# Edge scores of a graph attention layer: squares on ScalarE and a second product on TensorE for one of four chunks of dimensions

## The chip, the cores and the metric

One core of one Trainium2 chip. The metric is the device time of one launch in microseconds (us). TensorE, VectorE, ScalarE, GpSimd and SyncE run beside each other and meet at semaphores; sixteen DMA engines move data between HBM and the on-chip memory SBUF. TensorE writes to PSUM only.

## The reference, cut to what matters

The program is a block of a graph network: layer norm, a graph attention and a mixing term, and a mixture of experts. The change touches only the score of an edge in the graph attention (N = 2500 nodes, 80000 edges, 8 heads of 64 dimensions, 512 in all):

```python
def _gat_forward(x, edge_index, W_e, W_r, a):
    src = edge_index[0]
    dst = edge_index[1]
    h_e = jnp.einsum('nf,hfd->hnd', x, W_e)
    h_r = jnp.einsum('nf,hfd->hnd', x, W_r)
    a_src, a_dst, a_dif, a_abs, a_prd = jnp.split(a, 5, axis=1)
    s_src = jnp.einsum('hnd,hd->hn', h_e, a_src)[:, src]
    s_dst = jnp.einsum('hnd,hd->hn', h_e, a_dst)[:, dst]
    hr_src = h_r[:, src]
    hr_dst = h_r[:, dst]
    diff = hr_dst - hr_src
    score = s_src + s_dst + jnp.einsum('hed,hd->he', diff, a_dif) + jnp.einsum('hed,hd->he', jnp.abs(diff), a_abs) + jnp.einsum('hed,hd->he', hr_src * hr_dst, a_prd)
    alpha = jax.nn.leaky_relu(score, negative_slope=ALPHA)
```

With w = hr_dst - hr_src the product of the two rows is half of (hr_src^2 + hr_dst^2 - w^2). The two squares belong to the nodes and are put into tables beforehand. What is left for each edge, dimension and head is a_abs |w| - a_prd/2 w^2, which is -a_prd/2 (|w| - c) |w| with c = 2 a_abs / a_prd.

## The kernel before, in words

`score_edges` takes the edges, sorted by source node, in 336 groups of 256 (GROUP = 2 tiles of 128). For a group n, with its 512 dimensions in KF = 4 chunks of 128:

- GpSimd gathers the two tiles' target rows (512 dimensions and 8 head terms each) into `rows_v`, a ring of six (L1065). It waits for `summed` of six groups back.
- VectorE makes a one-hot matrix of source nodes, `source_onehot_t` (`locate`, L1094).
- TensorE expands the source rows with it into `ps_u`: for each tile two halves of 260 columns, in three bf16 parts each, 12 products in all (`expand`, L1133). A tile of `ps_u` is free once VectorE has subtracted from it in the group before.
- VectorE subtracts, in place in `rows_v`, one instruction for each tile (`differ`, L1100): this is w.
- TensorE transposes w, dimensions to partitions, in 8 pieces into `ps_w`, of which there is one (`transpose`, L1148). It waits for `abs_set` of the group before.
- ScalarE makes the magnitudes of all four chunks at once, `w_abs`, three buffers (`magnitudes`, L1178).
- VectorE makes z = (|w| - c) |w| with one instruction for each chunk (`multiply`, L1114; c is `corner`).
- TensorE sums over the dimensions of each head: for each chunk a product of `head_weight` (128x32, -a_prd/2 in the column of the head) with z, into that chunk's own strip of 32 PSUM partitions of `ps_heads`, and then for each of the two tiles a product that adds the head terms into strip 0 or 1 (`add_heads`, L1157 and L1160). It gives `summed`.
- ScalarE copies the scores out (`keep_scores`, L1183), and SyncE's queue writes them to HBM.

The order on each engine is written by hand: `in_turns` gives each step with how many groups it lags. The numbers set what stands behind what:

```python
in_turns(v, TURNS, ((2, differ_first), (2, differ_second), (4, multiply), (0, locate)), TURN)
in_turns(nc.tensor, TURNS, ((2, expand_first), (2, expand_second), (5, add_heads), (3, transpose)), TURN)
in_turns(sc, TURNS, ((9, magnitudes), (0, fetch_ids), (11, keep_scores)), TURN)
```

So TensorE goes, in turn m: expansion of group m-2, head sums of m-5, transposes of m-3; VectorE subtracts m-2, makes z of m-4, locates m.

Of the kernel before, what the change touches and what calls it, by code (L numbers as in the profile page):

```python
# [7 lines left out]
ALU = mybir.AluOpType  # L8
ACT = mybir.ActivationFunctionType
# [5 lines left out]
P = 128  # L15
L = 125
NB = N // L
KF = F // P
GROUP = 2
GE = GROUP * P  # L20
CHUNKS = P // HEADS
STRIP = P // KF
# [954 lines left out]
def score_edges(nc, a, const, edge, group_block, tab_v, parts, parts_in, scores, merged, keys, keys_in, local_ids):  # L977
# [7 lines left out]

    ident, row, col = const["ident"], const["row"], const["col"]
    BUFS, RING, TURN = 3, 6, 12
    ID_GROUPS, ID_SETS = 3, 4
    TURNS = GROUPS // TURN
    assert TURNS * TURN == GROUPS and GROUP == 2 and ID_GROUPS * ID_SETS == TURN  # L990
    HALF = EW // 2
    with ExitStack() as ctx:
        def sb(name, shape, dt=F32):
            return ctx.enter_context(nc.sbuf_tensor(name, shape, dt))
# [7 lines left out]
        def sbs(name, shape, dt=F32):  # L1002
            return [sb(f"{name}{h}", shape, dt) for h in range(BUFS)]
# [2 lines left out]
        ids = [sb(f"edge_ids{s}", [L, ID_GROUPS * GE], BF16) for s in range(ID_SETS)]  # L1006
        onehot_t = sbs("source_onehot_t", [L, GROUP, P], BF16)
        w, w_abs = rows, sbs("w_abs", [P, KF, GE])
        z = sbs("z", [P, KF, GE])
        score = sbs("score", [P, GE])  # L1010
        a_abs, prd, minus_prd = sb("a_abs", [P, KF]), sb("prd", [P, KF]), sb("minus_prd", [P, KF])
        tiny, corner = sb("tiny", [P, KF]), sb("corner", [P, KF])
        head_i, head_f = sb("head_i", [P, 1], I32), sb("head_f", [P, 1])
        head_sum, head_weight = sb("head_sum", [P, STRIP]), sb("head_weight", [P, KF, STRIP])
        ps_w = ps("ps_w", [P, KF, GE])
        ps_u = [ps(f"ps_u{j}", [P, 2, 512]) for j in range(GROUP)]

# [51 lines left out]
        def _(dve):  # L1069
            v = nc.vector  # L1070
# [11 lines left out]
            link(v.reciprocal(corner[:, :], prd[:, :]))  # L1082
            link(v.scalar_tensor_tensor(corner[:, :], corner[:, :], 2.0, a_abs[:, :], ALU.mult, ALU.mult))
            link(v.tensor_scalar(minus_prd[:, :], prd[:, :], -0.5, None, ALU.mult))
            for c in range(KF):
                ins = v.tensor_scalar(head_weight[:, c, :], head_sum[:, :], minus_prd[:, c:c + 1], None, ALU.mult)
            link(ins)
# [21 lines left out]
            def multiply(n, q, turn):  # L1109
                h = q % BUFS  # L1110
                at_least(dve, abs_set, n + 1)
                at_least(dve, summed, n - BUFS + 1)
                for c in range(KF):
                    ins = v.scalar_tensor_tensor(z[h][:, c, :], w_abs[h][:, c, :], corner[:, c:c + 1], w_abs[h][:, c, :], ALU.subtract, ALU.mult)  # L1114
                ins.then_inc(z_set, 1)

# [2 lines left out]
        @block.tensor  # L1119
        def _(pe):  # L1120
            pe.wait_ge(vectors_set, 1)
            pe.wait_ge(parts_in, 16 * PART_LOADS)

            block_of = {}

            def expand(n, q, j, b):

                at_least(pe, located, n + 1)
                at_least(pe, differed, n * GROUP + j - 1)
                for half in range(2):  # L1130
                    for part in range(PARTS):
                        rows_of_part = parts[:, DS(b, 1), part, half * HALF:(half + 1) * HALF].rearrange("p o c -> p (o c)")
                        ins = nc.tensor.matmul(ps_u[j][:, half, 0:HALF], onehot_t[q % BUFS][:, j, :], rows_of_part, start=part == 0, stop=part == PARTS - 1)  # L1133
                ins.then_inc(expanded, 1)

            def expand_first(n, q, turn):
                block_of[q] = pe.value_load(group_block[0:1, DS(n, 1)], min_val=0, max_val=NB - 1)
                expand(n, q, 0, block_of[q])

            def expand_second(n, q, turn):  # L1140
                expand(n, q, 1, block_of[q])

            def transpose(n, q, turn):
                at_least(pe, differed, n * GROUP + GROUP)
                at_least(pe, abs_set, n)
                for c in range(KF):
                    for j in range(GROUP):
                        ins = nc.tensor.transpose(ps_w[:, c, j * P:(j + 1) * P], w[q % RING][:, j, c * P:(c + 1) * P], ident[:, :])  # L1148
                ins.then_inc(turned, 1)

            def add_heads(n, q, turn):
                h = q % BUFS
                at_least(pe, z_set, n + 1)
                at_least(pe, score_kept, n - 1)
                for c in range(KF):
                    strip = ps_heads[q % 2][c * STRIP:(c + 1) * STRIP, 0:GE]
                    ins = nc.tensor.matmul(strip, head_weight[:, c, :], z[h][:, c, :], start=True, stop=True)  # L1157
                for j in range(GROUP):
                    strip = ps_heads[q % 2][j * STRIP:j * STRIP + HEADS, j * P:(j + 1) * P]
                    ins = nc.tensor.matmul(strip, w[q % RING][:, j, F:EW], ident[:, :], start=False, stop=True, skip_group_check=True)  # L1160
                ins.then_inc(summed, 1)

            in_turns(nc.tensor, TURNS, ((2, expand_first), (2, expand_second), (5, add_heads), (3, transpose)), TURN)

        @block.scalar
        def _(act):
# [7 lines left out]
            def magnitudes(n, q, turn):  # L1174
                h = q % BUFS
                at_least(act, turned, n + 1)
                at_least(act, z_set, n - BUFS + 1)
                sc.activation(w_abs[h][:, :, :], ps_w[:, :, :], ACT.Abs).then_inc(abs_set, 1)  # L1178

            def keep_scores(n, q, turn):  # L1180
                at_least(act, summed, n + 1)
# [812 lines left out]
```

## Time and profile before

| | |
|---|---|
| median of 3 runs | 3093.24 us (3088.78 to 3095.16) |
| the profiled execution's own time | 3089.13 us |
| its span, first to last instruction | 3087.2 us |
| mean granted TensorE clock | 0.923 |
| TensorE products busy | 2585.4 us (84%) |
| VectorE busy | 2339.1 us (76%) |
| GpSimd busy | 1500.3 us (49%) |
| ScalarE busy | 708.6 us (23%) |

The profile comes from one execution. PE is TensorE, PEld its weight loads, DVE VectorE, ACT ScalarE, POOL GpSimd. A busy time runs from an instruction's start to its end, latency included, and the ends of products are modelled; instructions of an engine can overlap at their ends. So two starts tell how fast an engine goes, and a duration tells when a result is there. In a timeline, instructions of one line that follow each other are merged: the row gives the first one's start, the time to the last one's end, and how many. Each f32 product has two records on TensorE. The stage that `score_edges` fills lies between about 580 and 1645 us.

### The profile page before, as it was taken

To read this page: it belongs to the slowest core of one execution; us is meant where nothing else is said; L and a number is where in the kernel's file an instruction comes from. 1 tells how busy PE (TensorE), PEld (TensorE's weight loads), DVE (VectorE), ACT (ScalarE), POOL (GpSimd) and SP (SyncE) were. 2 spreads that over 40 slices of the span, in tenths; PEclk is the share of its full clock that TensorE was granted. 3 is DMA by queue.
4 is the path that set the end of the run, shared out by engine and by line. 5 is a ranking of instruction groups with operands and counts; after the bars stand their busy time and mean duration, and the time that the engine had idled before them with its cause. 6 is when DMAs were issued, how large, how long until landed. Compare 5 with 4: busy or idle time off the path is not lost. (4 is left out here: it accounts for less than half of the span.)

```text
span 3087.2 us, 61474 instructions
## 1 busy us (share of the span) xinstructions
PE 2585.4 (84%) x16639; PEld 1699.8 (55%) x16640; DVE 2339.1 (76%) x4723; ACT 708.6 (23%) x1319; POOL 1500.3 (49%) x1562
## 2 busy tenths in 40 slices
PE   2399989599999999999992199999999998688990
PEld 2266654377777777777771154555555554675440
DVE  3567843499999999999998888888888888522111
ACT  0133331144444444444441100000000000331220
POOL 0233310366666666666660077777777776130113
PEclk6699989799999999999996599999999999689995
DMA  4012122777777777777774077777777776520224
GB/s 134 4 59 62 59 78 98 139 202 201 203 201 200 201 201 202 201 200 201 203 197 169 9 211 210 210 210 210 210 210 210 209 210 183 165 74 17 81 75 143
DMA packets 196487, 483.43 MB, mean 157 GB/s; under 512 B 51110, under 2 KB 81250, under 8 KB 195651
## 3 DMA queue, kind: packets, MB, share of 16 engines
q0 software_dynamic: 116400, 372.54, 44.5%
q1 hardware_dynamic: 55457, 84.04, 8.5%
q10 hardware_dynamic: 24562, 26.03, 2.6%
q8 instruction: 32, 0.52, 0.1%
q14 instruction: 36, 0.29, 0.0%
HBM read 435.38 MB, written 47.03 MB: 156 GB/s over the span
## 5 line engine op out<-in xcount | busy, mean ns | idle before, releaser
L1065 POOL DMA_INDIRECT rows_v<-target_rows,edge_dst x672 | 662.5, 986 | 413.5 <-PE ps_heads L1160 307.4
L1386 PE MATMUL ps_sum<-messages,node_onehot 128*125 128x512 f32 x1344 | 741.0, 640 | 77.6 <-DVE messages L1362 69.9
L1341 POOL DMA_INDIRECT rows_e<-message_rows,edge_dst x672 | 635.3, 945 | 346.4 <-issue 203.5
L1114 DVE SCALAR_TENSOR_TENSOR z<-w_abs,corner 128x256 f32<-128x256 f32 x1344 | 559.8, 478 | 1.3 <-ACT w_abs L1178 1.3
L1133 PE MATMUL ps_u<-edge_space,source_onehot_t 125*128 x4032 | 505.8, 275 | 32.9 <-DVE source_onehot_t L1094 28.6
L1178 ACT ACTIVATE w_abs<-ps_w 128x1024 f32<-128x1024 f32 x336 | 344.2, 1024 | 688.4 <-PE ps_w L1148 683.6
L1362 DVE TENSOR_TENSOR messages<-rows_e,ps_beside 128x1024 f32<-128x1024 f32 x336 | 410.2, 1221 | 103.4 <-DMA rows_e<-message_rows,edge_dst 97.8
L1100 DVE TENSOR_TENSOR rows_v<-rows_v,ps_u 128x520 f32<-128x520 f32 x672 | 456.1, 696 | 11.6 <-DMA rows_v<-target_rows,edge_dst 5.6
L1133 PEld LDWEIGHTS ps_u<-edge_space,source_onehot_t 125*128 125x128 bf16 x4032 | 393.6, 98 | 86.1 <-issue 34.4
L1387 PEld LDWEIGHTS ps_den<-edge_space,node_onehot 128*125 128x125 f32 x1344 | 253.1, 188 | 326.3 <-issue 326.3
L1148 PE MATMUL ps_w<-ident,rows_v 128*128 128x128 f32 x2688 | 367.3, 280 | 0.0
L1148 PEld LDWEIGHTS ps_w<-ident,rows_v 128*128 128x128 f32 x2688 | 287.7, 141 | 73.3 <-issue 72.3
L1386 PEld LDWEIGHTS ps_sum<-messages,node_onehot 128*125 128x125 f32 x1344 | 199.5, 188 | 104.8 <-DVE messages L1362 82.7
L1372 DVE TENSOR_TENSOR edge_space<-ps_sum,edge_space 125x512 f32 x336 | 229.5, 683 | 1.6 <-PE ps_den L1387 1.2
L1157 PE MATMUL ps_heads<-z,head_weight 128*32 128x256 f32 x2688 | 215.1, 392 | 2.6 <-DVE z L1114 2.6
L1401 ACT COPY ps_beside<-edge_space 128x96 f32 (+1 forms) x56 | 13.5, 243 | 805.6 <-DVE messages L1362 800.8
L1387 PE MATMUL ps_den<-edge_space,node_onehot 128*125 (+1 forms) x1344 | 189.5, 213 | 0.0
L1358 DVE TENSOR_TENSOR node_onehot<-ps_beside,edge_local 128x250 f32<-128x250 f32 x336 | 137.2, 408 | 0.4 <-ACT ps_beside L1401 0.4
L1799 DVE SCALAR_TENSOR_TENSOR swiglu_gate<-swiglu_gate,ps_up 128x256 f32<-128x256 f32 x27 | 11.4, 421 | 161.0 <-ACT swiglu_gate L1870 161.0
L354 POOL TENSOR_TENSOR squares<-row_v 125x512 f32<-125x512 f32 x20 | 20.9, 1044 | 228.6 <-ACT row_v L915 228.6
L1160 PE MATMUL ps_heads<-ident,rows_v 128*8 128x128 f32 x1344 | 130.8, 273 | 0.0
L1183 ACT COPY score<-ps_heads 128x256 f32<-128x256 f32 x336 | 123.0, 366 | 5.4 <-SPq L1053 3.6
(390 smaller groups left out, 2606.5 us busy)
## 6 DMA issues: line engine op xcount, KB each, us to landing
scores<-score SPq DMA_DIRECT2D x1344, 8.0 KB
edge_ids<-local_ids ACTq DMA_DIRECT2D x112, 187.5 KB
edge_space<-in_L_ffn_w_dram SPq DMA_DIRECT2D x24, 512.0 KB, 4.4
rows_v<-target_rows,edge_dst POOLq DMA_INDIRECT x672
rows_e<-message_rows,edge_dst POOLq DMA_INDIRECT x672, 3.7
source_parts<-edge_space SPq DMA_DIRECT2D x20, 380.9 KB
edge_space<-source_parts SPq DMA_DIRECT2D x4, 1904.3 KB
token_rows_out<-token_y SPq DMA_DIRECT2D x27, 256.0 KB, 2.8
```

The costliest lines, as they stand in the source:

```text
L1065: nc.gpsimd.indirect_dma_start(rows[q][:, j, :], None, tab_v, bass.IndirectOffsetOnAxis(ap=edge["dst"][:, tile:tile + 1], axis=0)).then_in ...
L1100: v.tensor_tensor(w[q % RING][:, j, :].rearrange("p (a b) -> p a b", a=2), rows[q % RING][:, j, :].rearrange("p (a b) -> p a b", a=2), ps_ ...
L1114: ins = v.scalar_tensor_tensor(z[h][:, c, :], w_abs[h][:, c, :], corner[:, c:c + 1], w_abs[h][:, c, :], ALU.subtract, ALU.mult)
L1133: ins = nc.tensor.matmul(ps_u[j][:, half, 0:HALF], onehot_t[q % BUFS][:, j, :], rows_of_part, start=part == 0, stop=part == PARTS - 1)
L1148: ins = nc.tensor.transpose(ps_w[:, c, j * P:(j + 1) * P], w[q % RING][:, j, c * P:(c + 1) * P], ident[:, :])
L1157: ins = nc.tensor.matmul(strip, head_weight[:, c, :], z[h][:, c, :], start=True, stop=True)
L1178: sc.activation(w_abs[h][:, :, :], ps_w[:, :, :], ACT.Abs).then_inc(abs_set, 1)
L1341: nc.gpsimd.indirect_dma_start(rows[q][:, j, :], None, tab_e, bass.IndirectOffsetOnAxis(ap=edge["dst"][:, tile:tile + 1], axis=0)).then_in ...
L1362: v.tensor_tensor(messages[h][:, :, :].rearrange("p j (h d) -> p (j h) d", d=D), rows[q % RING][:, :, :].rearrange("p j (h d) -> p (j h) d ...
L1372: v.tensor_tensor(total, ps_sum[q % BUFS][:, :], total, ALU.add)
L1386: nc.tensor.matmul(ps_sum[h][:, :], onehot[h][:, j, :], messages[h][:, j, :], start=j == 0, stop=j == GROUP - 1)
L1387: ins = nc.tensor.matmul(ps_den[h][:, 0:HEADS], onehot[h][:, j, :], tile_weights[:, DS(n * GROUP + j, 1), :].rearrange("p o h -> p (o h)") ...
```

## The change

Of the four chunks the last (SQUARED = 1) is no longer factored. ScalarE makes |w| of all four chunks as before and then w^2 of the last chunk in a second instruction; `abs_set` comes after both. VectorE makes z for three chunks. TensorE adds, in the last chunk's strip, `head_weight` times the squares and then a new `abs_weight` (a_abs in the column of the head) times the magnitudes. Since TensorE now reads `w_abs`, ScalarE waits for `summed` of three groups back before it writes there, where it waited for `z_set`.

```diff
+    SQUARED = 1
+    FACTORED = KF - SQUARED
...
-        z = sbs("z", [P, KF, GE])
+        z, w_square = sbs("z", [P, FACTORED, GE]), sbs("w_square", [P, SQUARED, GE])
...
+            for c in range(FACTORED, KF):
+                v.tensor_scalar(abs_weight[:, c - FACTORED, :], head_sum[:, :], a_abs[:, c:c + 1], None, ALU.mult)
...
-                for c in range(KF):
+                for c in range(FACTORED):
                     ins = v.scalar_tensor_tensor(z[h][:, c, :], w_abs[h][:, c, :], corner[:, c:c + 1], w_abs[h][:, c, :], ALU.subtract, ALU.mult)
...
-                    ins = nc.tensor.matmul(strip, head_weight[:, c, :], z[h][:, c, :], start=True, stop=True)
+                    if c < FACTORED:
+                        nc.tensor.matmul(strip, head_weight[:, c, :], z[h][:, c, :], start=True, stop=True)
+                    else:
+                        nc.tensor.matmul(strip, head_weight[:, c, :], w_square[h][:, c - FACTORED, :], start=True, stop=False)
+                        nc.tensor.matmul(strip, abs_weight[:, c - FACTORED, :], w_abs[h][:, c, :], start=False, stop=True)
...
-                at_least(act, z_set, n - BUFS + 1)
-                sc.activation(w_abs[h][:, :, :], ps_w[:, :, :], ACT.Abs).then_inc(abs_set, 1)
+                at_least(act, summed, n - BUFS + 1)
+                sc.activation(w_abs[h][:, :, :], ps_w[:, :, :], ACT.Abs)
+                sc.activation(w_square[h][:, :, :], ps_w[:, FACTORED:KF, :], ACT.Square).then_inc(abs_set, 1)
```

TensorE's order in one turn of the loop, before (with what a row waits for; lines L1133 expansion, L1157 and L1160 head sums, L1148 transposes, L1137 the next turn's table entry):

```order
L1133 MATMUL ps_u<-edge_space,source_onehot_t 128x260 [waits differed,located]
L1133 MATMUL ps_u<-edge_space,source_onehot_t 128x260 x5
L1157 MATMUL ps_heads<-z,head_weight 32x256 [waits score_kept,z_set]
L1157 MATMUL ps_heads<-z,head_weight 32x256 x3
L1160 MATMUL ps_heads<-ident,rows_v 8x128 x2
L1148 MATMUL ps_w<-ident,rows_v 128x128 [waits abs_set,differed]
L1148 MATMUL ps_w<-ident,rows_v 128x128 x7
L1137 TENSOR_LOAD group_block
```

The same turn now (expansion L1137, head sums L1162 to L1168, transposes L1152):

```order
L1137 MATMUL ps_u<-edge_space,source_onehot_t 128x260 [waits differed,located]
L1137 MATMUL ps_u<-edge_space,source_onehot_t 128x260 x5
L1162 MATMUL ps_heads<-z,head_weight 32x256 [waits score_kept,z_set]
L1162 MATMUL ps_heads<-z,head_weight 32x256 x2
L1164 MATMUL ps_heads<-w_square,head_weight 32x256
L1165 MATMUL ps_heads<-w_abs,abs_weight 32x256
L1168 MATMUL ps_heads<-ident,rows_v 8x128 x2
L1152 MATMUL ps_w<-ident,rows_v 128x128 [waits abs_set,differed]
L1152 MATMUL ps_w<-ident,rows_v 128x128 x7
L1141 TENSOR_LOAD group_block
```

Four products of 32x256 have become five; the fourth and the fifth write the same strip. Nothing else has moved.

ScalarE's order in the same loop, before (two turns):

```order
L1178 ACTIVATE w_abs<-ps_w 128x1024 [waits z_set,w_turned]
L1183 COPY score<-ps_heads 128x256 [waits score_free,summed]
L93 REGISTER_ALU
L1178 ACTIVATE w_abs<-ps_w 128x1024 [waits z_set,w_turned]
L1172 ISA [waits located]
```

And now:

```order
L1186 ACTIVATE w_abs<-ps_w 128x1024 [waits summed,w_turned]
L1187 ACTIVATE w_square<-ps_w 128x256
L1192 COPY score<-ps_heads 128x256 [waits score_free,summed]
L1186 ACTIVATE w_abs<-ps_w 128x1024 [waits summed,w_turned]
L1187 ACTIVATE w_square<-ps_w 128x256
L1180 DMA edge_ids<-local_ids 125x768 [waits located]
```

The squares stand between the magnitudes and the score copy of two groups before, without a wait of their own, and there is no table load in the loop.

## Rows read from the trace of the kernel before

**Rows 1.** The page, busy us (share of the span) and instructions.

```profile
PE 2585.4 (84%) x16639; PEld 1699.8 (55%) x16640; DVE 2339.1 (76%) x4723; ACT 708.6 (23%) x1319; POOL 1500.3 (49%) x1562
```

**Rows 2.** The page, busy tenths and granted clock in 40 slices of the span.

```profile
PE   2399989599999999999992199999999998688990
...
DVE  3567843499999999999998888888888888522111
...
PEclk6699989799999999999996599999999999689995
```

**Rows 3.** Busy time of each engine in one stretch, 700 to 1600 us.

```profile
core 0: us, PE busy (x) PEld busy (x) DVE busy (x) ACT busy (x) POOL busy (x), PEclk, DMA share, GB/s
700.00:1600.00 900.00, 900.00 (x9209) 673.55 (x9206) 900.00 (x2014) 370.68 (x576) 565.94 (x576) 1.00 0.75 201
```

**Rows 4.** Groups of instructions by line, 700 to 1600 us, shapes kept apart.

```profile
line engine op names shapes xcount | busy us, mean ns | idle before us <-releasers
...
L1114 DVE SCALAR_TENSOR_TENSOR z<-w_abs,corner 128x256 f32<-128x256 f32 x1150 | 479.1, 478 | 0.0
...
L1148 PE MATMUL ps_w<-ident,rows_v 128*128 128x128 f32 x2297 | 313.7, 280 | 0.0
L1178 ACT ACTIVATE w_abs<-ps_w 128x1024 f32<-128x1024 f32 x288 | 295.0, 1024 | 530.5 <-PE ps_w L1148 530.5
...
L1157 PE MATMUL ps_heads<-z,head_weight 128*32 128x256 f32 x2304 | 184.0, 391 | 0.0
...
L1183 ACT COPY score<-ps_heads 128x256 f32<-128x256 f32 x288 | 105.5, 366 | 0.0
```

**Rows 5.** Who waited for whom, 700 to 1600 us: total, times, longest.

```profile
ACT w_abs L1178 <- PE ps_w L1148: 530.5, 288, 1.9
POOL rows_v L1065 <- PE ps_heads L1160: 245.2, 288, 0.9
...
PEld ps_w L1148 <- issue: 62.7, 287, 0.2
PEld ps_heads L1157 <- issue: 61.6, 288, 0.2
```

**Rows 6.** Timeline of TensorE's products, 1199.8 to 1203.7: start, us, what.

```profile
1199.56 1.09 PE L1148 MATMUL ps_w<-ident,rows_v 128*128 128x128 f32 x8
1200.49 1.49 PE L1133 MATMUL ps_u<-edge_space,source_onehot_t 125*128 x12
1201.92 0.64 PE L1157 MATMUL ps_heads<-z,head_weight 128*32 128x256 f32 x8
1202.37 0.39 PE L1160 MATMUL ps_heads<-ident,rows_v 128*8 128x128 f32 x4
1202.69 1.09 PE L1148 MATMUL ps_w<-ident,rows_v 128*128 128x128 f32 x8
```

**Rows 7.** The same in narrow windows: last expansion, second head pass, second identity pass.

```profile
1201.71 0.27 PE L1133 MATMUL ps_u<-edge_space,source_onehot_t 125*128 x1
...
1202.16 0.40 PE L1157 MATMUL ps_heads<-z,head_weight 128*32 128x256 f32 x4
...
1202.48 0.28 PE L1160 MATMUL ps_heads<-ident,rows_v 128*8 128x128 f32 x2
```

**Rows 8.** Timeline of VectorE, 1199.8 to 1204.5.

```profile
1199.51 1.67 DVE L1114 SCALAR_TENSOR_TENSOR z<-w_abs,corner 128x256 f32<-128x256 f32 x4
1201.09 0.28 DVE L1094 TENSOR_SCALAR source_onehot_t<-edge_ids,iota_col 125x256 bf16<-125x256 bf16 x1
1201.36 1.36 DVE L1100 TENSOR_TENSOR rows_v<-rows_v,ps_u 128x520 f32<-128x520 f32 x2
1202.64 1.67 DVE L1114 SCALAR_TENSOR_TENSOR z<-w_abs,corner 128x256 f32<-128x256 f32 x4
```

**Rows 9.** Timeline of VectorE in a narrow window: the second subtraction.

```profile
1202.02 0.70 DVE L1100 TENSOR_TENSOR rows_v<-rows_v,ps_u 128x520 f32<-128x520 f32 x1
```

**Rows 10.** Timeline of ScalarE, 1199.8 to 1204.9.

```profile
1200.77 1.02 ACT L1178 ACTIVATE w_abs<-ps_w 128x1024 f32<-128x1024 f32 x1 [1.92 <-PE ps_w L1148]
...
1201.69 0.37 ACT L1183 COPY score<-ps_heads 128x256 f32<-128x256 f32 x1
```

More of the change, by code:

```diff
@@ L1013, in score_edges @@
         head_i, head_f = sb("head_i", [P, 1], I32), sb("head_f", [P, 1])
-        head_sum, head_weight = sb("head_sum", [P, STRIP]), sb("head_weight", [P, KF, STRIP])
+        head_sum, head_weight, abs_weight = sb("head_sum", [P, STRIP]), sb("head_weight", [P, KF, STRIP]), sb("abs_weight", [P, SQUARED, STRIP])
         ps_w = ps("ps_w", [P, KF, GE])
```

## The prediction, made before the changed kernel ran

> **What bounds the kernel now.** I read the views in this order: the page's shares and slices, the busy time of the scoring stage, its groups of instructions, its waits, and then one period of TensorE, VectorE and ScalarE instruction by instruction.
>
> The page says only that TensorE is busy for 84% of the span [rows 1] and that TensorE and VectorE are both full in slices 8 to 21 [rows 2]; the change lies wholly in that stage. In the 900 us from 700 to 1600 both are busy for all 900 us, at a granted clock of 1.00, with a DMA share of 0.75 [rows 3]. The reader should see that this cannot say which of the two sets the pace. Group counts give the period: 288 `w_abs` activations in 900 us [rows 4], so 900 / 288 = 3.125 us for each group of 256 edges, and there are 336 groups. The waits name only ScalarE and GpSimd waiting for TensorE, and weight loads that wait for nothing the profile shows [rows 5]. So DMA, ScalarE and GpSimd have room.
>
> TensorE against VectorE has to be read from starts, because a busy time includes an instruction's latency. TensorE's period [rows 6]: eight transposes start at 1199.56, twelve expansions at 1200.49, the head products at 1201.92, the two identity products at 1202.37, the next transposes at 1202.69: 0.93 + 1.43 + 0.45 + 0.32 = 3.13 us. Inside it nothing is loose [rows 7]: the twelfth expansion starts at 1201.71, so eleven intervals take 1.22 us, 0.111 each; from the last expansion to the first head product are 0.21 us, its own 0.11 and 0.10 more; the second pass of the head products starts at 1202.16, 0.24 after the first; the second pass of the identity products starts at 1202.48, and the transposes 0.21 later, again 0.11 of streaming and 0.10 more. The two steps of 0.10 stand where TensorE goes from full-width products to products in 32-column strips and back.
>
> Are those 0.10 waits for somebody? The head products need `z` of a group whose last VectorE product ended at 1199.51 + 1.67 = 1201.18 [rows 8], 0.74 us before. The transposes at 1202.69 need the `w_abs` activation that ran from 1200.77 to 1201.79 [rows 10], 0.90 us before. So TensorE waits for nobody. VectorE does: of the two subtractions the first starts at 1201.36 and the second at 1202.02 [rows 8, 9], 0.66 apart, while the second is followed by the next product after 1202.64 - 1202.02 = 0.62; the second one needs the expansion whose last product ran from 1201.71 to 1201.98 [rows 7]. VectorE waits there some 0.05 us in each period. **TensorE sets the pace, and VectorE is only 0.05 us behind it.**
>
> **The change, part by part.**
>
> *VectorE product gone.* One of four at L1114. Four take 1.58 us from first start to the following instruction [rows 8], 0.396 each. VectorE then needs 3.13 - 0.05 - 0.40 = 2.68 us a group. It was not the bound, so this is worth nothing; what was the cover is now idle time.
>
> *TensorE product added.* The fourth chunk now takes two products in the same strip, squares with `head_weight` and magnitudes with `abs_weight`, 128x256 f32 each. The trace has two passes for each f32 product (eight records of L1157 for the four products of a group: 2304 in 288 groups [rows 4]), the four strips side by side. A pass that follows another in its strip takes 0.21 us, from 1202.16 to 1202.37 [rows 7, 6]. Products of the same strip can't run side by side, so strip 3 gets two more passes, from 1202.37 to 1202.79. The identity products are in strips 0 and 1 and took 0.22 us for two passes; they run beside the first of these. What follows, the transposes, uses the full array and starts 0.10 us after the last strip is through: 1202.89 in place of 1202.69. Per group 0.42 - 0.22 = 0.20 to 0.21 us; I take 0.21, for the finer reading 2 x 0.215 - 0.22.
> The weight load of `abs_weight` is 128x32 like the head weights' and lies under a pass of 0.21.
> Bounds for this term: at least 0.16, if half of the 0.10 at the switch back to full width can lie under the longer strip; 0.31, if the identity products' weight loads are held back behind strip 3 so that they begin a load of 0.10 after its last pass has begun; 0.43, if nothing overlaps.
> The Trainium skill, page "TensorE: Matmul & The Clock Gate", Part 3 (What overlaps and what doesn't), says that products start and end in program order while only weight loads are pulled ahead. By that rule the identity products, which come behind strip 3's second product, would start at its last pass, 1202.58, and end their 0.22 at 1202.80 in place of 1202.79: 0.22 us a group. Nothing in the trace of before has a busy strip ahead of a free one, so no row decides between the two.
>
> *ScalarE square added.* Its nearest row is the copy at L1183, also 128x256 out of PSUM: 0.37 us [rows 4]. An activation is followed 0.92 us after its start [rows 10], so the squares run from 1201.69 to 1202.06, and `abs_set` now comes at 1202.06 in place of 1201.79. TensorE's next transposes need it at 1202.69, 0.63 us later, VectorE's next product at 1202.64. Both are still in time. Bounds: nothing, and 1.02 as for the large activation; even that ends at 1202.71, before the new 1202.89. ScalarE's sum is 1.02 + 0.37 + 0.37 = 1.76 us of 3.3. The score copy behind it moves 0.37 later; it frees a bank that TensorE needs one period on. Cost 0.
>
> *Waits moved.* ScalarE now waits for `summed` of three groups back, where it waited for `z_set`. In TensorE's order the add of that group stands a whole period ahead of the activation. Cost 0. The one small VectorE multiplication ahead of the loop costs under 1 us. GpSimd's gathers wait for TensorE already [rows 5] and get slower with it; DMA has more room.
>
> *Sum.* 336 x 0.21 = 70.6 us. The profiled execution took 3089.13 us (its span is 3087.2): 3089.1 + 70.6 = 3159.7. The median of the runs shown lies 4.1 us above that execution, so I forecast 3163.8, rounded to 3164.
>
> **The rivals.**
>
> *A. VectorE is the bound after all: faster.* TensorE's busy time is modelled, and its weight loads are busy for only 673.55 of 900 us [rows 3]. If 0.61 us or more of TensorE's period were loose, 0.21 of it would hide the new passes and the period would fall by VectorE's 0.40: 336 x 0.40 = 133 us, 2960 us. The point from which it decides: every 0.01 us of looseness beyond 0.21 gives 3.4 us back below today's time. Against it stands that TensorE's starts fill 3.13 of 3.125 us and only 0.20 of that, the two switches, isn't streaming, and that VectorE waits for TensorE while TensorE's operands are 0.7 to 0.9 us early. Chance 0.06.
> The Trainium skill, page "Perfetto Trace Analysis", section "Identifying the Most-Contended Engine", speaks for this rival: a matmul's busy share is no measure of TensorE's headroom, and the busy share of weight loads should be used for it. That share is 75% here, which would call a quarter of the period loose, 0.78 us, and so give A in full, 2960 us. The order of starts above says otherwise, and I weigh it higher.
>
> *B. No overlap, slower still.* The identity products wait until strip 3 is free: 336 x 0.43 = 144 us, 3238 us; or with weight loads held back 336 x 0.31 = 104 us, 3197 us. For it: the trace shows no case of a strip that is busy twice as long as its neighbours. Against it: weight loads for the identity products already slip in beside running passes. Chance 0.09 for both, mostly for the milder.
>
> *C. The added passes cost nothing.* If the two switches were waits in disguise they could swallow 0.20 us: 3093 us. Against it is that no operand is late at either. Chance 0.03.
>
> *D. ScalarE's chain takes over.* Transposes, magnitudes and squares, then the transposes of the next group, all through one `ps_w`: it would need squares of over 1.2 us, for instance by a table load in the loop, and neither copy nor activation has anything of the kind beside it. Chance 0.01.
>
> **How the numbers follow.** The forecast has 0.81. The range runs from the lower bound of the term, 336 x 0.16 = 54 us or 3147, to the milder form of B with 3 us of spread between runs, 3200. A and C lie outside, and so does the hard form of B, together 0.13. Taking 0.2% (6 us) as what a measurement of this kernel can tell from no change: faster 0.06, which is A; same 0.03, which is C; slower 0.91, the forecast, B and D.
>
> **What would show it.** In the profile after, between 700 and 1600 us, some 270 groups instead of 288, a period of 3.33 us. TensorE's head products take two more pass starts 0.21 apart, and 0.97 us from their first start to the transposes in place of 0.77. VectorE falls to about 80% busy and gets an idle time before L1104's subtractions, released by TensorE's `ps_u`, 0.6 us a group or 200 us over the stage. The squares take 0.37 us each and nothing waits for them. The stage ends some 70 us later, and every stage behind it is as long as before. The forecast is wrong if the period is 3.13 or less, if TensorE shows idle time released by ScalarE or VectorE, or if the gap from the last head pass to the identity products grows.

## The result and the profile after

The changed kernel takes **3166.33 us** (3164.71 to 3166.62) against 3093.34 us before (3088.78 to 3095.16): a ratio of 1.0237, 95% interval 1.0219 to 1.0255. The forecast was 3164 in a range of 3147 to 3200. The profiled execution took 3166.62 us, its span is 3164.6 us.

The page after, busy us and instructions, and the slices (columns as in [rows 1, 2]):

```profile
PE 2659.1 (84%) x17311; PEld 1722.0 (54%) x17312; DVE 2211.2 (70%) x4388; ACT 801.2 (25%) x1655; POOL 1503.1 (47%) x1562
...
PE   2399988599999999999997069999999998688991
...
DVE  3567833488888888888887988888888888622111
...
PEclk6699989799999999999998589999999999679995
```

TensorE has 672 more records, two f32 passes in each of 336 groups, and stays full over the stage; VectorE has its 336 products less (one of them is made up for by the multiplication ahead of the loop) and shows 8 where it had 9. Over the stage the granted clock is 9 in both, and 1.00 in the rows of 700 to 1600 us.

Busy time of each engine between 700 and 1600 us (columns as in [rows 3]):

```profile
700.00:1600.00 900.00, 900.00 (x9119) 646.02 (x9117) 736.68 (x1609) 419.78 (x807) 532.02 (x537) 1.00 0.71 187
```

VectorE has gone from 900.00 to 736.68 us, 82%. TensorE's weight loads have gone down although it has more to do: fewer groups pass, and for each group they have gone up, from 673.55 / 288 = 2.34 us to 646.02 / 269 = 2.40.

Groups of instructions of the same stretch (columns as in [rows 4]):

```profile
L1104 DVE TENSOR_TENSOR rows_v<-rows_v,ps_u 128x520 f32<-128x520 f32 x537 | 365.6, 696 | 163.8 <-PE ps_u L1137 117.5 <-issue 46.3
L1118 DVE SCALAR_TENSOR_TENSOR z<-w_abs,corner 128x256 f32<-128x256 f32 x804 | 340.5, 479 | 0.0
...
L1186 ACT ACTIVATE w_abs<-ps_w 128x1024 f32<-128x1024 f32 x269 | 275.5, 1024 | 482.0 <-PE ps_w L1152 482.0
...
L1164 PE MATMUL ps_heads<-w_square,head_weight 128*32 128x256 f32 x536 | 165.9, 391 | 0.0
L1165 PE MATMUL ps_heads<-w_abs,abs_weight 128*32 128x256 f32 x536 | 159.4, 379 | 0.0
...
L1187 ACT ACTIVATE w_square<-ps_w 128x256 f32<-128x256 f32 x269 | 101.6, 378 | 0.0
```

The magnitudes count 269 groups where there were 288 [rows 4]: 900 / 269 = 3.346 us a group; the middle distance between the starts of successive groups' transposes is 3.355 us where it was 3.129. VectorE's subtractions now have 163.8 us of idle time before them, 0.61 us a group.

TensorE's timeline, one head sum and the transposes behind it (start us, us, what):

```profile
1200.68 0.42 PE L1162 MATMUL ps_heads<-z,head_weight 128*32 128x256 f32 x3
1200.70 0.40 PE L1164 MATMUL ps_heads<-w_square,head_weight 128*32 128x256 f32 x1
1200.92 0.39 PE L1162 MATMUL ps_heads<-z,head_weight 128*32 128x256 f32 x3
1200.94 0.38 PE L1164 MATMUL ps_heads<-w_square,head_weight 128*32 128x256 f32 x1
1201.14 0.28 PE L1168 MATMUL ps_heads<-ident,rows_v 128*8 128x128 f32 x2
1201.16 0.38 PE L1165 MATMUL ps_heads<-w_abs,abs_weight 128*32 128x256 f32 x1
1201.25 0.28 PE L1168 MATMUL ps_heads<-ident,rows_v 128*8 128x128 f32 x2
1201.37 0.38 PE L1165 MATMUL ps_heads<-w_abs,abs_weight 128*32 128x256 f32 x1
1201.68 1.09 PE L1152 MATMUL ps_w<-ident,rows_v 128*128 128x128 f32 x8
```

Strip 3 has four passes, at 1200.70, 1200.94, 1201.16 and 1201.37; the identity products fill two short ones beside it. From the first head pass to the transposes are 1.00 us where there were 0.77 [rows 6]. The period has grown by as much: from 3.129 to a mean of 3.356, by 0.227 us.

VectorE's, GpSimd's and ScalarE's timelines around it (in brackets the idle time before and who ended it):

```profile
1200.13 1.36 DVE L1104 TENSOR_TENSOR rows_v<-rows_v,ps_u 128x520 f32<-128x520 f32 x2 [0.61 <-PE ps_u L1137]
1201.40 1.27 DVE L1118 SCALAR_TENSOR_TENSOR z<-w_abs,corner 128x256 f32<-128x256 f32 x3
```

```profile
1202.06 1.04 POOL L1067 DMA_INDIRECT rows_v<-target_rows,edge_dst  x1 [1.07 <-PE ps_heads L1168]
```

```profile
1200.38 0.38 ACT L1187 ACTIVATE w_square<-ps_w 128x256 f32<-128x256 f32 x1
```

VectorE now waits for the expansion. GpSimd's gather is released by the head sums' signal 1.38 us after their first start (1200.68 to 1202.06). The transposes still don't wait for ScalarE: the squares end at 1200.38 + 0.38 = 1200.76, 0.92 us before them.

### The profile page after: what moved, and what is told of

It is laid out like the page before. It is cut to its first block and busy times, and to the rows that moved or that the text cites. A ratio compares the mean times of both kernels' runs of the same rounds, so it can differ in the third digit from the quotient of the medians.

```text
span 3164.6 us, 62819 instructions
## 1 busy us (share of the span) xinstructions
PE 2659.1 (84%) x17311; PEld 1722.0 (54%) x17312; DVE 2211.2 (70%) x4388; ACT 801.2 (25%) x1655; POOL 1503.1 (47%) x1562
## 5 line engine op out<-in xcount | busy, mean ns | idle before, releaser
L1137 PE MATMUL ps_u<-edge_space,source_onehot_t 125*128 x4032 | 504.1, 274 | 37.7 <-DVE source_onehot_t L1098 37.7
L1137 PEld LDWEIGHTS ps_u<-edge_space,source_onehot_t 125*128 125x128 bf16 x4032 | 393.0, 97 | 89.9 <-issue 38.8
L1118 DVE SCALAR_TENSOR_TENSOR z<-w_abs,corner 128x256 f32<-128x256 f32 x1008 | 426.9, 479 | 2.7 <-ACT w_square L1187 2.7
L1152 PE MATMUL ps_w<-ident,rows_v 128*128 128x128 f32 x2688 | 366.9, 279 | 0.6 <-ACT w_square L1187 0.4
L1152 PEld LDWEIGHTS ps_w<-ident,rows_v 128*128 128x128 f32 x2688 | 287.2, 141 | 138.4 <-DVE rows_v L1104 126.4
L1162 PE MATMUL ps_heads<-z,head_weight 128*32 128x256 f32 x2016 | 212.5, 391 | 1.6 <-DVE z L1118 1.6
L1164 PE MATMUL ps_heads<-w_square,head_weight 128*32 128x256 f32 x672 | 208.0, 391 | 0.0
L1165 PE MATMUL ps_heads<-w_abs,abs_weight 128*32 128x256 f32 x672 | 199.9, 379 | 0.0
L1168 PE MATMUL ps_heads<-ident,rows_v 128*8 128x128 f32 x1344 | 130.5, 273 | 0.0
```

## The experiments

These ran in three sets: e1 to e4, then e7, e8, e5 and e6, then a1, e9, e10 and e11. The runs' records give chip 3 for the first and the third set and chip 6 for the second. They name no chip for the two kernels above; from the times I take it to be another, and call it the first. In the three sets the kernel before takes 3354.85, 3393.23 and 3363.49 us, so each time is to be read against that of its own set. Most of the difference has nothing to do with the change. It lies behind the scoring stage: from the last group's transposes to the end are 1450.2 us in the kernel before on the first chip and 1659.1 in e1. There the GB/s row of the page reads 209 to 211 in the kernel after above, and about 164 to 174 in e1:

```profile
GB/s 130 6 59 62 65 83 77 163 189 188 188 186 187 188 188 188 188 188 187 186 189 183 63 132 210 210 210 210 209 210 211 209 209 202 162 83 11 80 80 140
```

```profile
GB/s 123 11 62 63 63 103 97 179 192 191 191 191 190 191 191 191 190 192 191 189 156 39 172 165 164 167 165 171 165 174 168 165 171 169 154 122 4 73 77 138
```

In e1 the granted clock is 0.87 there (1860 to 2700 us), with TensorE busy for 663.43 of 840 us. On the first chip it is 1.00. No run tells whether slower transfers or something else is the cause.

But the scoring stage differs too, and that matters below. I therefore read the period beside the time: the distances between the first transposes of successive groups between 630 and 1680 us (in the kernel before, whose last transposes start at 1637, without the last and short distance), their middle value, mean and, where it is another, the value that only a twentieth lies below.

| kernel | period: middle / mean (low) | time, us | ratio to before, 95% |
|---|---|---|---|
| before, first chip | 3.129 / 3.129 | 3093.34 | |
| changed, first chip | 3.355 / 3.356 | 3166.33 | 1.0237 (1.0219 to 1.0255) |
| changed again, a1 | 3.356 / 3.361 | 3387.02 | 1.0079 (1.0062 to 1.0096) |
| e1 square alone | 3.296 / 3.296 (3.203) | 3356.11 | 1.0005 (0.9993 to 1.0017) |
| e2 product alone | 3.356 / 3.375 | 3390.95 | 1.0109 (1.0091 to 1.0128) |
| e3 VectorE's product away | 3.203 / 3.271 (3.128) | 3348.18 | 0.9977 (0.9962 to 0.9991) |
| e4 product split over strips | 3.267 / 3.306 (3.142) | 3357.55 | 1.0007 (0.9991 to 1.0022) |
| e7 strip 3 first | 3.336 / 3.343 | 3400.02 | 1.0022 (1.0008 to 1.0036) |
| e8 two chunks squared | 3.362 / 3.370 | 3406.37 | 1.0045 (1.0022 to 1.0067) |
| e9 buffers freed early | 3.285 / 3.290 (3.204) | 3361.08 | 0.9993 (0.9983 to 1.0003) |
| e10 e9 and e3 | 3.237 / 3.273 (3.128) | 3355.24 | 0.9975 (0.9960 to 0.9989) |

### The parts of the change

**e1: only ScalarE's squares**, into a buffer that nobody reads, with the moved wait.

```diff
-                at_least(act, z_set, n - BUFS + 1)
-                sc.activation(w_abs[h][:, :, :], ps_w[:, :, :], ACT.Abs).then_inc(abs_set, 1)
+                at_least(act, summed, n - BUFS + 1)
+                sc.activation(w_abs[h][:, :, :], ps_w[:, :, :], ACT.Abs)
+                sc.activation(w_square[h][:, :, :], ps_w[:, KF - 1:KF, :], ACT.Square).then_inc(abs_set, 1)
```

> The kernel before with ScalarE's squares of the fourth chunk added and its wait moved to summed, VectorE's four products and TensorE's four kept; the squares are used by nobody. Theory (TensorE alone sets the pace, the loss is strip 3's two extra passes): no change, 3093 us, period 3.125 us. Rival (the later abs_set or the moved wait holds TensorE's transposes or VectorE back): up to 336 x 0.23 = 77 us more, 3170, with TensorE or VectorE idle, released by ScalarE.

Measured 1.0005, an interval that holds 1. The squares and the moved wait cost nothing. On this chip VectorE sets the pace of most groups (see e9). For the first chip the reading is the one above: the squares end 0.92 us before the transposes that need them.

**e2: only TensorE's fifth product**, in strip 3 with a weight of zeros, and the moved wait of e1; VectorE keeps its four products.

```diff
...
+                nc.tensor.matmul(strip, zero_weight[:, :], w_abs[h][:, KF - 1, :], start=False, stop=True)
...
```

> The kernel before with only TensorE's fifth head product added, in strip 3, magnitudes times a weight of zeros, and all four VectorE products kept. Theory: the whole loss of the change, 336 x 0.227 = 76 us, so 3169 us; VectorE's fourth product was worth nothing, so keeping it costs nothing (it needs 3.07 us of a period of 3.35). Rival (VectorE's relief gave something back in the change, or VectorE is close to the bound): slower than the changed kernel, over 3175 us.

Measured: TensorE's timeline in e2,

```profile
1200.30 1.09 PE L1150 MATMUL ps_w<-ident,rows_v 128*128 128x128 f32 x8
...
1202.65 0.64 PE L1159 MATMUL ps_heads<-z,head_weight 128*32 128x256 f32 x8
1203.11 0.28 PE L1163 MATMUL ps_heads<-ident,rows_v 128*8 128x128 f32 x2
1203.13 0.38 PE L1160 MATMUL ps_heads<-w_abs,zero_weight 128*32 128x256 f32 x1
...
1203.34 0.38 PE L1160 MATMUL ps_heads<-w_abs,zero_weight 128*32 128x256 f32 x1
1203.65 0.55 PE L1150 MATMUL ps_w<-ident,rows_v 128*128 128x128 f32 x3
```

The transposes are 1203.65 - 1200.30 = 3.35 us apart and the middle period is 3.356, that of the changed kernel to a thousandth. The product alone makes it, with or without VectorE's fourth. In time e2 costs 1.0109, 36 us and not the 76 expected; a1 and e9 below show why. It is also more than a1's 1.0079, of another set on this chip: its mean period is 3.375 against 3.361, so with all four VectorE products some groups are late besides.

**e3: only VectorE's product away**, with the moved wait of e1. Three z, and TensorE uses `w_abs` in the fourth strip.

```diff
-                for c in range(KF):
+                for c in range(KF - 1):
...
+                    factor = z[h] if c < KF - 1 else w_abs[h]
...
```

> The kernel before without VectorE's product for the fourth chunk: TensorE multiplies its head weights with the magnitudes instead, so the fourth chunk's quadratic part is left out of the scores. TensorE has as many products as before. Theory: no gain beyond 3 us, 3090 to 3093 us, VectorE idle for 0.45 us a group. Rival (VectorE was the bound): 336 x 0.40 = 133 us less, 2960 us.

Measured: 0.9977, 7 us less and not 133. TensorE's timeline where the stage runs at its fastest, and VectorE's:

```profile
1202.71 1.09 PE L1148 MATMUL ps_w<-ident,rows_v 128*128 128x128 f32 x8
...
1205.84 1.09 PE L1148 MATMUL ps_w<-ident,rows_v 128*128 128x128 f32 x8
```

```profile
1204.51 0.69 DVE L1100 TENSOR_TENSOR rows_v<-rows_v,ps_u 128x520 f32<-128x520 f32 x1 [0.37 <-PE ps_u L1133]
1206.04 0.69 DVE L1100 TENSOR_TENSOR rows_v<-rows_v,ps_u 128x520 f32<-128x520 f32 x1 [0.83 <-PE ps_u L1133]
```

The transposes are 3.13 us apart while VectorE stands idle for 0.37 and 0.83: with 0.40 us less VectorE work in each group the quickest groups take 3.128, what nearly every group took before on the first chip. None of e3's is quicker. That is TensorE's own floor, and rival A falls for the first chip, where the kernel before already ran at it. On this chip 45% of e3's groups go at it and 1% of e1's, so here VectorE's product does hold groups back.

### The size of the product's cost

**e4: the changed kernel with the magnitudes' product cut in two halves** of 128 edges, in strips 3 and 2, so that each of the four strips has two long and two short passes.

```diff
...
-                        nc.tensor.matmul(strip, abs_weight[:, c - FACTORED, :], w_abs[h][:, c, :], start=False, stop=True)
...
+                        for j in range(GROUP):
+                            half = ps_heads[q % 2][(KF - 1 - j) * STRIP:(KF - j) * STRIP, j * P:(j + 1) * P]
+                            nc.tensor.matmul(half, abs_weight[:, c - FACTORED, :], w_abs[h][:, c, j * P:(j + 1) * P], start=False, stop=True, skip_group_check=True)
```

> The changed kernel with the magnitudes' product cut in two halves of 128 edges, the first in strip 3 and the second in strip 2. Each strip then has 256 columns of head product and 128 more, as strips 0 and 1 have with their identity products. Theory (the cost is the longest strip, not the number of passes): each half takes two passes of 0.11 us beside the identity products, the period goes back to 3.13 to 3.16 us and the time to 3093 to 3103 us. Rival (every added pass or weight load costs TensorE time of its own): 3150 us or more.

TensorE's timeline in e4:

```profile
1201.05 1.09 PE L1152 MATMUL ps_w<-ident,rows_v 128*128 128x128 f32 x8
...
1203.41 0.42 PE L1162 MATMUL ps_heads<-z,head_weight 128*32 128x256 f32 x3
...
1203.88 0.28 PE L1167 MATMUL ps_heads<-w_abs,abs_weight 128*32 128x128 f32 x2
...
1203.98 0.28 PE L1167 MATMUL ps_heads<-w_abs,abs_weight 128*32 128x128 f32 x2
1204.19 0.98 PE L1152 MATMUL ps_w<-ident,rows_v 128*128 128x128 f32 x7
```

From the first head pass to the transposes 0.78 us instead of 1.00, and the lowest periods are 3.142: the same arithmetic as in the changed kernel costs 0.014 us over TensorE's floor of 3.128, instead of 0.227, when it is spread over strips. The cost is the length of the longest strip. On this chip the ratio of 1.0007 to before says that the loss is gone; it doesn't say that anything is won. The mean period of 3.306 is that of e1 and e9 and not 3.142, for reasons that come with e9.

**e7: the changed kernel with strip 3's products issued first**, `for c in reversed(range(KF))`.

> The changed kernel with the four chunks issued in reverse, so that strip 3 with its two products begins first. Theory: strip 3's passes start some 0.02 us later than strip 0's only because they are issued last; issued first, the period loses up to 0.02 us, 336 x 0.02 = 7 us, so 3159 us against 3166. Rival (a product that waits for its strip holds those behind it): the other three strips' products start only when strip 3's second product has begun, 0.45 us later, and the time is over 3250 us.

TensorE's timeline in e7:

```profile
1203.14 0.40 PE L1164 MATMUL ps_heads<-w_square,head_weight 128*32 128x256 f32 x1
1203.16 0.42 PE L1162 MATMUL ps_heads<-z,head_weight 128*32 128x256 f32 x3
...
1203.82 0.38 PE L1165 MATMUL ps_heads<-w_abs,abs_weight 128*32 128x256 f32 x1
1204.12 0.55 PE L1152 MATMUL ps_w<-ident,rows_v 128*128 128x128 f32 x3
```

Strip 3 now leads by 0.02 where it trailed by 0.02; from the first head pass to the transposes are 0.98 us, and the period is 3.336. The expected 0.02 is there, read against the changed kernel's 3.355 and 3.356 on the two other chips; on this chip the changed kernel itself wasn't run. The absolute time that the text expected was for the first chip and doesn't apply.

**e8: SQUARED = 2**, so strip 2 too has four passes instead of two, and VectorE makes only two products.

> The changed kernel with SQUARED = 2: two chunks by squares, strips 2 and 3 with two products each, VectorE with two products less than before. Theory (the longest strip counts, and strips 2 and 3 run side by side): no slower than with one, 3166 us, although there are two more passes and weight loads; VectorE idle for 1 us a group. Rival (each added pass costs of its own): another 336 x 0.2 = 70 us, 3240 us. Rival (VectorE's work counts): faster than 3166.

Busy time in e8, 700 to 1600 us, and its timeline of TensorE:

```profile
700.00:1600.00 900.00, 900.00 (x9627) 647.34 (x9616) 635.52 (x1335) 474.75 (x801) 504.46 (x534) 1.00 0.71 187
```

```profile
1205.36 0.39 PE L1165 MATMUL ps_heads<-w_abs,abs_weight 128*32 128x256 f32 x2
...
1205.58 0.39 PE L1165 MATMUL ps_heads<-w_abs,abs_weight 128*32 128x256 f32 x2
```

Two strips go through their added passes side by side (x2 at each start), and the period grows from 3.355 to 3.362: a second added product costs 0.007 us where the first cost 0.227. VectorE is down to 635.52 of 900 us and the kernel is no faster: 6 us slower than e7, which has one chunk squared, in the same set.

### The same change on another chip

**a1: the changed kernel as it is.**

> The changed kernel once more, beside the others on their chip. On the chips of the earlier experiments the kernel before took 3355 and 3393 us in place of 3093, and its scoring stage was no longer at TensorE's pace all the way: score copies waited for the score writes of SyncE's queue. Theory: TensorE's own period is 3.355 us here too, but the stage of the kernel before already takes some 3.28 us a group on such a chip, so the change costs about 336 x 0.08 = 27 us, a ratio of 1.01; on a chip where the kernel before takes 3093 us the ratio is 1.024 again. Rival (the loss scales with the chip): 1.024 on any chip.

Measured +24 us, ratio 1.0079, at a period of 3.356. The changed kernel's period is the same on both chips; it is the kernel before whose period is another: its near relatives e1 and e9, both within 0.1% of it in time, have 3.296 and 3.290. The kernel before itself has no trace there. 336 x (3.361 - 3.290) = 24 us. So the product's 0.227 us is all there, but some 0.16 of it fills time that was already lost. What is it lost to?

**e9: the kernel before, with each score buffer freed one group after its write** rather than three together, by SyncE:

```diff
...
+                if h or not first:
+                    sp.wait_ge(score_out[(h - 1) % BUFS], t * (16 * KF) + (16 * KF if h else 0))
+                    sp.sem_inc(score_free, 1)
...
-                for h in range(BUFS):
-                    sp.wait_ge(score_out[h], t * (16 * KF) + 16 * KF)
-                    sp.sem_inc(score_free, 1)
...
```

> The kernel before with each score buffer given free when the next group's writes are issued, instead of three together after the third has landed. Theory (on the slower chips the copies' wait for the score writes is what holds the stage over TensorE's 3.13 us): on such a chip the period goes from 3.28 to 3.13 us, 336 x 0.15 = 50 us less, ratio 0.985; on a chip of 3093 us nothing. Rival (late gathers or HBM hold it): no change anywhere.

Measured 0.9993. My theory, that slow score writes hold the stage, falls. e9's own timelines of VectorE, GpSimd and TensorE show another thing:

```profile
1192.14 1.66 DVE L1121 SCALAR_TENSOR_TENSOR z<-w_abs,corner 128x256 f32<-128x256 f32 x4
1193.73 0.28 DVE L1101 TENSOR_SCALAR source_onehot_t<-edge_ids,iota_col 125x256 bf16<-125x256 bf16 x1
1193.92 0.69 DVE L1107 TENSOR_TENSOR rows_v<-rows_v,ps_u 128x520 f32<-128x520 f32 x1
1194.84 0.70 DVE L1107 TENSOR_TENSOR rows_v<-rows_v,ps_u 128x520 f32<-128x520 f32 x1 [0.23 <-PE ps_u L1140]
1195.45 1.67 DVE L1121 SCALAR_TENSOR_TENSOR z<-w_abs,corner 128x256 f32<-128x256 f32 x4
```

```profile
1193.17 1.06 POOL L1072 DMA_INDIRECT rows_v<-target_rows,edge_dst  x1 [0.30 <-issue]
```

```profile
1192.29 1.50 PE L1140 MATMUL ps_u<-edge_space,source_onehot_t 125*128 x12
1193.86 0.64 PE L1164 MATMUL ps_heads<-z,head_weight 128*32 128x256 f32 x8
```

The second subtraction starts 0.92 us after the first, where it was 0.66 [rows 8, 9], and the loop on VectorE, 0.19 + 0.92 + 0.61 + 1.59 = 3.31 us, is as long as the period. TensorE's head products start at 1193.86, 0.06 us after VectorE's products ended (1192.14 + 1.66 = 1193.80). On the first chip that distance was 0.74 in every group of the kernel before between 700 and 1600 us. In e9 it is under 0.12 in 83% of the groups of that stretch, in e1 in 82%. So here VectorE sets the pace in most groups, and TensorE waits for it. From its last expansion to the head products are 0.35 us in e9 (middle value) and 0.20 in the kernel before on the first chip. These 0.15 us are nearly all of the 0.16 that the added product fills in a1. The subtraction isn't late for TensorE's sake, though the profile names `ps_u`: the last expansion had ended at 1192.29 + 1.50 = 1193.79, 1.05 us before it. All this fits e1 and a1. It doesn't explain by itself why e3 gains so little.

**e10: e9 and e3 together**, to see whether the two hide each other.

> The kernel of the run before this one without VectorE's product for the fourth chunk (TensorE takes the magnitudes there; the chunk's quadratic part is left out of the scores). With the score writes out of the way only TensorE and VectorE can set the pace. Theory: the same time as the run before this one within 4 us, period 3.13 us, VectorE at 85%. Rival (VectorE's product is worth something): up to 133 us less.

Measured 3355.24, 6 us below e9, and not at a period of 3.13 as expected. VectorE's work is 0.40 us a group shorter and the mean period only 0.017. Some 30% of the groups go at 3.13; the others don't. Part of the reason is that the second subtraction comes later still. Counted from the moment when its expansion has ended and the first subtraction has had its 0.61 us, it starts 0.27 us late on average in e9, 0.42 in e3 and 0.49 in e10 (groups between 700 and 1600 us), so in e10 half of the 0.40 goes there. Who holds the rest I have not settled. The change's cost on the first chip doesn't depend on it.

### Trying to win more

The two steps of 0.10 us, where TensorE goes into the strips and back, come once each in a group. Doing the head sums of two groups back to back, every second turn, should halve them.

```diff
...
+            def add_pair(n, q, turn):
+                if q % 2:
+                    add_heads(n - 1, q - 1, turn)
+                    add_heads(n, q, turn)
...
```

**e5** does it to e4's kernel, **e6** to the kernel before, **e11** to e5 with e9's freeing and a ring of eight gather buffers.

> The split of the magnitudes' product, and head sums of two groups made back to back in every second turn instead of one in each. TensorE then changes between full-width and strip products once in two groups; each change was read as 0.10 us and there were two in a group. Theory: 0.10 us less a group, period 3.03 us, 336 x 0.10 = 34 us below the kernel before, 3060 us, with VectorE (2.68 us) still behind. Rival (the 0.10 are weight loads or waits that come with each group): 3093 to 3100 us. Rival (GpSimd's gathers, which wait for summed, come too late for the even groups): slower than 3093.

> The kernel before with head sums of two groups back to back and nothing else. TensorE gets 0.10 us a group shorter, but VectorE needs 3.07 us. Theory: the gain stops at VectorE, 0.05 us a group, 336 x 0.05 = 17 us, 3076 us, VectorE without idle and TensorE waiting for it. If it gains 34 us as with the split, my reading of VectorE's need is wrong.

> The paired head sums once more, with what held them back taken away: split magnitudes' product, early freeing of score buffers, and a ring of 8 gathered groups in place of 6 (the loop body is 24 groups long instead of 12 and fetches node numbers for 6 groups at a time). Theory (two changes between full-width and strip products cost 0.20 us, once in two groups now; the 700 us lost in the paired runs were gathers that came late): period 3.03 to 3.05 us, 27 to 34 us below the kernel with early freeing, ratio to the kernel before 0.990 on a fast chip and 0.975 on a slow one. Rival (gathers are still late with two more buffers): slower than the kernel before, VectorE idle for gathers.

All three miss by far: 4117.9 us (ratio 1.2162, 1.2116 to 1.2207), 3923.61 us (1.1551, 1.1520 to 1.1581) and 4126.11 us (1.2264, 1.2236 to 1.2292). Waits in e5, 800 to 1600 us (total, times, longest):

```profile
POOL rows_v L1067 <- PE ps_heads L1170: 455.8, 72, 7.5
DVE rows_v L1104 <- remote: 350.7, 78, 5.6
```

GpSimd waits for the delayed sums in pieces of up to 7.5 us and VectorE behind it for something off the core's engines. I took that for gathers that start too late for a ring of six; with eight buffers, in e11, the same waits stay (464.5 us in pieces of up to 11.4, and 339.8), so this is not the cause, or not the only one. It stays open, and so does what a switch into the strips would give back. No kernel with the full scores is faster than the kernel before by more than its interval; e4 equals it. e3 and e10, which leave out a part, are 0.2 to 0.3% faster.

## Why the prediction was right

**TensorE sets the pace: right** for the first chip, and shown. e2 adds only TensorE's product and has the changed kernel's period; e8 takes away a second VectorE product and gains nothing; e3 without the fourth goes no faster than 3.128, which is the period that the kernel before had there. The argument from starts, no loose time between them and no late operand, held.

**VectorE's product worth nothing: right.** Its 0.40 us has become idle time, 0.61 us a group against the "0.6" forecast, 163.8 us in the 900 shown and 207 over the stage, at 82% busy ("about 80%"). One reading was off, with no effect on the sum: I put VectorE's wait at 0.05 us a period, from the second subtraction alone. The first one waits too: it starts 0.27 us after the one-hot instruction [rows 8], while in e9, with TensorE not in the way, it starts 0.19 after (1193.73 to 1193.92). VectorE was some 0.12 us behind TensorE, not 0.05. On the chip of e1 and e9 the order of the two engines is another: VectorE sets the pace of most groups in these two, which are close to the kernel before, and its product is worth a little there, 7 us in e3.

**TensorE's product, 0.21 us: right in kind, 0.017 too small.** Passes follow each other by 0.21 to 0.22 as in the term. Left out was that strip 3's passes begin 0.02 later than strip 0's, since they are issued last, so that the chain of four ends 0.02 later than four passes of strip 0 would; e7 puts them first and gets the 0.02 back. 336 x 0.227 = 76 us against 70.6 forecast; the profiled spans differ by 77.4, the medians by 73.

That the forecast of 3164 lies only 2.3 us from the 3166.33 measured is in part luck. The 70.6 were 5.7 us too small for the period. The 4.1 us by which the median before lay above its profiled execution were added, and after the change the median lies 0.3 below it. The profiled executions also differ by something that isn't the change: the stage's first transposes come at 591.7 us after and at 583.6 before, and the kernel before has one hole of 6 us after its sixth group that the changed one hasn't; the two nearly cancel.

**The rule on program order.** By the sentence from the Trainium skill, page "TensorE: Matmul & The Clock Gate", Part 3, the identity products would have begun only with strip 3's last pass. The trace does not agree as to starts: they are issued last and begin at 1201.14, before the first pass of the magnitudes' product at 1201.16. The ends in the profile are modelled and decide nothing. What does seem to come in order is the signal. GpSimd's gathers in the kernel before, around the period of [rows 6]:

```profile
1201.16 1.03 POOL L1065 DMA_INDIRECT rows_v<-target_rows,edge_dst  x1 [0.30 <-issue]
1203.04 0.94 POOL L1065 DMA_INDIRECT rows_v<-target_rows,edge_dst  x1 [0.85 <-PE ps_heads L1160]
```

The second of these waits on the last identity product. It came 1.12 us after the first head pass (1201.92 [rows 6] to 1203.04) and comes 1.38 after now, in nearly every group between 700 and 1600 us, though the identity products themselves begin 0.45 to 0.46 after that pass in both.

**Rival A: fell** on the first chip (e3's floor, e8). With it fell the busy share of weight loads, read as a measure of looseness, from the page "Perfetto Trace Analysis" of the Trainium skill, section "Identifying the Most-Contended Engine", which names the reached share of peak arithmetic beside it: weight loads were busy for 673.55 of 900 us [rows 3] and yet 0.227 us more of products made the period 0.227 us longer. **Rival B: fell**; identity products and magnitudes run side by side. **Rival C: fell** with the result, and **D** with e1 and the timelines: squares of 0.378 us, and nobody waits for them. The score copy behind them moves by 0.26 us (1200.38 to 1200.64), not by the 0.37 of the text.

**Waits moved, 0: right** (e1). The stages behind are as long as before: 1450.3 us from the last transposes to the end, and 1450.2 before.

What the forecast couldn't know is that its ratio holds for one chip: where other things already stretch the kernel before to 3.29 us, the same change costs 24 us and not 73.

## What to carry to other kernels

Where TensorE runs small products in strips side by side, an added product costs what it adds to the longest strip: 0.227 us when it lengthened one, 0.007 beside one that was as long, 0.014 when it was cut and spread. When two engines are both shown as 100% busy, put the starts of one period in a row for each and ask at every step whether an operand was late. Here the work taken from the engine whose operands were late was worth nothing. And a margin between two engines of 0.12 us in 3.13 was gone on another chip, where their order had turned, so name the margin beside the forecast.

## What was unexpected of the hardware

- Identity products that are later in the program start before an earlier product whose strip is still busy, while the signal behind them seems to wait for it (above).
- VectorE's second subtraction is late on the other chips, and not for TensorE's sake. In e9, between 700 and 1600 us, it starts 1.02 us (middle value) after its last expansion has ended; in the kernel before on the first chip it is 0.04. A gather runs beside it: in e9 from 1193.17 to 1194.23, with the second subtraction 0.61 us after its end, and all 266 pairs of that stretch that are over 0.72 us apart had a gather running at the first one's start. But a running gather isn't enough. On the first chip, before the change, 282 of the 288 groups had one too, begun some 0.20 us ahead, and the second subtraction started while it ran (1202.02 [rows 9]; the gather shown above ends at 1202.19). Nor does it hang on how far ahead the gather begins: in e8 152 pairs had it less than 0.21 us ahead, and were 0.9 us late. The Trainium skill, page "SBUF — State Buffer", section "Who interferes with whom", describes a port that VectorE and GpSimd share and lock against each other, and says that a VectorE instruction with at most one input in SBUF, outside the 2-port modes, does not contend with GpSimd. The subtraction has one input in SBUF and one in PSUM, so by that sentence the port is not the cause. No run tests it; the delay was seen, and its cause is open.
- The same kernel takes 3093 us in the first runs, and 3355 to 3393 in the later sets on the chips numbered 3 and 6.
